# A two-layer graph network's message stage: TensorE's looped program written out straight, the hidden layer two groups ahead, fixed buffers for gathered rows

## The reference

```python
src, dst, x = ...            # 212,500 edges sorted by dst, 12,500 nodes, x: 12500 x 64
Wxh = x @ Wl.T + bl                                   # layer 0
h = silu(edge_attr @ Wf1.T + bf1)                     # edge_attr: 212500 x 64
f = h @ Wf2.T + bf2
agg = segment_sum(f * Wxh[dst], src, 12500)
x = layernorm(x + layernorm(x + agg) * gamma + beta)
agg = segment_sum(x[src] * edge_weight[:, None], dst, 12500)   # layer 1
x = layernorm(x + relu((agg + x) @ W1 + b1) @ W2 + b2)
```

## Time and profile before

| | |
|---|---|
| time, median of 3 runs | 4407.96 us (4403.15 to 4412.23) |
| profiled execution, its own time | 4366.64 us |
| its span, first to last instruction | 4364.9 us |
| VectorE, TensorE, GpSimd, ScalarE busy | 62%, 58%, 55%, 20% |
| first and last start of a scatter | 151.6 us, 3057.2 us |

### The profile page before, as it was taken

One profiled execution on the slowest core, in us unless ns is written; L12 is line 12 of the kernel. 1 busy time (PEld: TensorE's weight loads), 2 busy tenths in 40 slices (PEclk: granted clock), 3 DMA queues, 4 the chain that ended last, 5 costly groups with the idle time before them and its releaser, 6 DMA issues. The chain is left out here.

```text
span 4364.9 us, 81175 instructions
## 1 busy us (share of the span) xinstructions
PE 2517.8 (58%) x28074; PEld 2052.6 (47%) x28075; DVE 2725.6 (62%) x5354; ACT 888.6 (20%) x1671; POOL 2381.8 (55%) x2228
## 2 busy tenths in 40 slices
PE   3565665555565565665555655555475166666775
PEld 3454444444444444444444444444464155555763
DVE  5555555555555555555555555555566899997776
ACT  2111111111111111111111111111111355551002
POOL 0466666566565665655656656656122655554452
PEclk9677777777677676767767777776798555558998
DMA  7422222222222222222222222221686199999992
GB/s 213 96 68 68 68 68 63 64 69 67 61 70 64 65 71 61 69 66 61 68 67 61 69 65 67 69 61 51 234 332 250 57 306 303 305 306 354 406 406 96
DMA packets 205906, 585.25 MB, mean 134 GB/s; under 512 B 57272, under 2 KB 74432, under 8 KB 193216
## 3 DMA queue, kind: packets, MB, share of 16 engines
q1 hardware_dynamic: 134016, 369.03, 27.5%
q0 software_dynamic: 68336, 213.37, 13.4%
q10 hardware_dynamic: 3408, 0.92, 0.1%
HBM read 389.22 MB, written 194.13 MB: 134 GB/s over the span
## 5 line engine op out<-in xcount | busy, mean ns | idle before, releaser
L1019 POOL DMA_INDIRECT region_rows<-x_space,pos x1664 | 1797.4, 1080 | 1128.2 <-DVE x_space L972 632.2
L972 DVE TENSOR_TENSOR x_space<-rest,x_space 128x512 bf16<-128x512 f32 x208 | 144.0, 692 | 1010.2 <-issue 628.0
L886 PEld LDWEIGHTS ps_fx<-tmp_space,window 128*128 128x128 bf16 x9984 | 483.1, 116 | 532.1 <-issue 528.7
L868 PE MATMUL ps_rank<-onehot,tri 128*128 128x98 bf16 x1664 | 160.2, 265 | 872.0 <-DVE onehot L907 866.9
L886 PE MATMUL ps_fx<-tmp_space,window 128*128 x9984 | 521.7, 218 | 241.5 <-issue 238.9
L868 PEld LDWEIGHTS ps_rank<-onehot,tri 128*128 128x128 bf16 x1664 | 118.6, 128 | 933.2 <-DVE onehot L907 927.6
L880 PE MATMUL ps_th<-in_t,w_wf 128*128 128x512 f32 x416 | 424.6, 1124 | 0.0
L823 ACT ACTIVATE hid_t<-ps_th,w_bf 128x512 f32<-128x512 f32 x208 | 143.0, 687 | 1162.4 <-remote 699.4
L894 PE MATMUL ps_fx<-w_wf,hid_t 128*128 128x128 f32 x1664 | 318.5, 342 | 40.2 <-issue 35.9
L894 PEld LDWEIGHTS ps_fx<-w_wf,hid_t 128*128 128x128 f32 x1664 | 268.6, 240 | 55.8 <-issue 55.2
L818 ACT COPY in_t<-ps_th 128x512 f32<-128x512 f32 x208 | 121.9, 586 | 767.5 <-PE ps_th L861 551.5
(11 more groups left out here) (232 smaller groups left out, 4776.5 us busy)
## 6 DMA issues: line engine op xcount, KB each, us to landing
tmp_space<-region_rows SPq DMA_DIRECT2D x98, 882.0 KB, 6.6
run_rows<-agg SPq DMA_DIRECT2D x98, 873.0 KB
x_space<-key_rows SPq DMA_DIRECT2D x98, 576.0 KB
x_space<-rbf SPq DMA_DIRECT2D x208, 256.0 KB
rel_bc<-rel_rows SPq DMA_DIRECT2D x208, 256.0 KB
region_rows<-x_space,pos POOLq DMA_INDIRECT x1664
region_rows<-x_space SPq DMA_DIRECT2D x1, 14259.0 KB, 73.5
wxh_rows<-agg POOLq DMA_DIRECT2D x1, 3328.0 KB, 23.3
```

What stands on the lines that cost most here:

```text
L868: e.matmul(ps_rank[:, 0:NB], tri[:, :], onehot[j % 2][:, t, :], start=(t == 0), stop=(t == T - 1))
L886: last = e.matmul(ps_x[:, t * D:(t + 1) * D], window_t[:, h, t * P:(t + 1) * P], wxh[:, bass.ds(b + h, 1), c, :].rearrange("p b d -> p (b ...
L1019: e.indirect_dma_start(out=region_rows, out_offset=bass.IndirectOffsetOnAxis(ap=pos[j][:, t:t + 1], axis=0), in_=rows_f[j][:, t, :], in_of ...
```

## The change

Four things change in `sorted_messages`, all the rest stays.

1. TensorE's program is written out for all 208 groups instead of looping over passes.
2. Two small buffers, `near` and `sides`, two of each, are filled by ScalarE for a group (`nearby`): the six rows of parts of the two `wxh` blocks that the group needs (384 bf16 for each partition), and its 16 values of `ind`. TensorE's L886 and L874 products read these at fixed addresses. `nearby` reads the block number into a register on ScalarE.
3. TensorE's order for group g becomes: block products of g, node rows of g, transposes of g + 1, output layer of g, hidden layer of g + 1. ScalarE's becomes: `high_part` and `middle_part` of g, then `nearby`, `inputs` and `hidden` of g + 2.
4. VectorE's bias step (`filters`) is moved from the start of a group to behind `positions` of the group before.

```diff
@@ sorted_messages @@
-            found = carve(0, (S, T * RW // 2), (S, T * D), (2, T, D))
+            found = carve(0, (S, T * RW // 2), (S, T * D), (2, T, D), (2, PARTS * D), (2, T))
...
+            near = [a.bitcast(BF16) for a in found[2 * S + 2:2 * S + 4]]
+            sides = [a.bitcast(BF16).rearrange("p (t k) -> p t k", k=2) for a in found[2 * S + 4:2 * S + 6]]
...
+            def after(body, i, j, by=1):
+
+                body(i + (j + by) // S, (j + by) % S)
@@ block.scalar @@
-                    seed(e, ev, si, hw, mw)
+                    seed(e, ev, si, hw, mw, nr, sd)
+
+                    def nearby(i, j):
+                        b = e.value_load(base_i[0:1, bass.ds(i * S + j, 1)], min_val=0, max_val=NB - 1)
+                        e.wait_ge(xw, count_of(i, j, 2))
+                        e.copy(near[j % 2], wxh[:, bass.ds(b, 2), :, :].rearrange("p b c d -> p (b c d)")).then_inc(nr, 1)
+                        e.wait_ge(rk, count_of(i, j, 2))
+                        e.copy(sides[j % 2], ind[:, tiles(i, j), :]).then_inc(sd, 1)
...
-                    def steady(i, j):
-                        after(inputs, i, j)
+                    def parts(i, j):
                         high_part(i, j)
-                        after(hidden, i, j)
                         middle_part(i, j)
+
+                    for j in range(2):
+                        nearby(0, j)
+                        inputs(0, j)
+                        hidden(0, j)
+                    with e.Fori(0, passes - 1) as i:
+                        for j in range(S):
+                            parts(i, j)
+                            after(nearby, i, j, 2)
+                            after(inputs, i, j, 2)
+                            after(hidden, i, j, 2)
...
@@ block.tensor: the loop's body is split into functions and reordered @@
-                    with e.Fori(0, passes) as i:
-                        for j in range(S):
-                            b = e.value_load(base_i[0:1, bass.ds(i * S + j, 1)], min_val=0, max_val=NB - 1)
...
+                    def blocks(i, j, b):
...
+                        e.wait_ge(sd, count_of(i, j))
+                        for t in range(T):
+                            last = e.matmul(ps_pairs[0:NB, bass.ds(b, 2)], onehot[j % 2][:, t, :], sides[j % 2][:, t, :],
+                                            start=False, stop=False)
+                        last.then_inc(rk, 1)
+
+                    def nodes(i, j):
+                        e.wait_ge(nr, count_of(i, j))
+                        e.wait_ge(m, count_of(i, j, 1))
+                        e.wait_ge(wi, count_of(i, j))
+                        for t in range(T):
+                            for h in range(2):
+                                for c in range(PARTS):
+                                    last = e.matmul(
+                                        ps_x[:, t * D:(t + 1) * D], window_t[:, h, t * P:(t + 1) * P],
+                                        near[j % 2][:, (h * PARTS + c) * D:(h * PARTS + c + 1) * D],
+                                        start=(h == 0 and c == 0), stop=(h == 1 and c == PARTS - 1))
+                        last.then_inc(xw, 1)
...
+                    def steady(i, j, ahead):
+                        b = e.value_load(base_i[0:1, i * S + j:i * S + j + 1], min_val=0, max_val=NB - 1)
+                        blocks(i, j, b)
+                        nodes(i, j)
+                        if ahead:
+                            after(inputs, i, j)
+                        outputs(i, j)
+                        if ahead:
+                            after(hidden, i, j)
 
                     inputs(0, 0)
                     hidden(0, 0)
+                    for i in range(passes):
                         for j in range(S):
+                            steady(i, j, i * S + j + 1 < NG)
@@ block.vector @@
-                    def products(i, j):
+                    def filters(i, j):
                         e.wait_ge(m, count_of(i, j, 1))
                         e.wait_ge(f2, count_of(i, j))
                         e.tensor_tensor(f_s[:, :, :], ps_f[:, :].rearrange("p (t d) -> p t d", d=D),
                                         wts["bf2"][:, None, :].broadcast_to([P, T, D]), ALU.add).then_inc(f1, 1)
+
+                    def products(i, j):
                         e.wait_ge(hw, count_of(i, j, 2))
...
                         after(positions, i, j)
+                        after(filters, i, j)
```

More of the change, by code:

```diff
@@ L786, in sorted_messages @@
             gate = only_if(sorted_i, True)
-            def after(body, i, j):
-                body(i + (j + 1) // S, (j + 1) % S)
+            def after(body, i, j, by=1):
+                body(i + (j + by) // S, (j + by) % S)
             with nc.Block() as block:
@@ L854, in _ @@
                     e.matmul(ps_pairs[0:NB, 0:NBP], zeros[:, 0:NB], zeros[:, 0:NBP], start=True, stop=False).then_inc(f_zero, 1)
-                    with e.Fori(0, passes) as i:
-                        for j in range(S):
-                            b = e.value_load(base_i[0:1, bass.ds(i * S + j, 1)], min_val=0, max_val=NB - 1)
[L858 to L895, removed]
-                            last.then_inc(f2, 1)
@@ new lines, in inputs, with hidden @@
+                    def inputs(i, j):
+                        e.wait_ge(ld[j], i * 16 + 16)
+                        e.wait_ge(ev, count_of(i, j, 1))
+                        for t in range(T // 2):
+                            last = e.transpose(ps_t[:, t * P:(t + 1) * P],
+                                               rbf_s[j][:, t * P:(t + 1) * P], ident[:, :])
+                        last.then_inc(tr, 1)
+                    def hidden(i, j):
+                        e.wait_ge(si, count_of(i, j, 1))
+                        e.wait_ge(ev, count_of(i, j))
+                        e.matmul(ps_h[:, :], wts["wf1"][:, :], in_t[:, :], start=True, stop=True).then_inc(h1, 1)
@@ new lines, in blocks @@
+                    def blocks(i, j, b):
+                        e.wait_ge(rn, count_of(i, j, 1))
+                        e.wait_ge(oh, count_of(i, j))
+                        for t in range(T):
+                            e.matmul(ps_rank[:, 0:NB], tri[:, :], onehot[j % 2][:, t, :],
+                                     start=(t == 0), stop=(t == T - 1))
+                        for t in range(T):
+                            e.matmul(ps_cnt[:, 0:NB], ones[:, :], onehot[j % 2][:, t, :],
+                                     start=(t == 0), stop=(t == T - 1))
+                        e.wait_ge(sd, count_of(i, j))
+                        for t in range(T):
+                            last = e.matmul(ps_pairs[0:NB, bass.ds(b, 2)], onehot[j % 2][:, t, :], sides[j % 2][:, t, :],
+                                            start=False, stop=False)
+                        last.then_inc(rk, 1)
@@ new lines, in outputs @@
+                    def outputs(i, j):
+                        e.wait_ge(f1, count_of(i, j, 1))
+                        e.wait_ge(si, count_of(i, j))
+                        for t in range(T // 2):
+                            last = e.matmul(ps_f[:, t * P:(t + 1) * P], hid_t[:, t * P:(t + 1) * P],
+                                            wts["wf2"][:, :], start=True, stop=True)
+                        last.then_inc(f2, 1)
+                    def steady(i, j, ahead):
[7 more added lines that the diff above has]
+                            after(hidden, i, j)
@@ L897, in _ @@
+                    inputs(0, 0)
+                    hidden(0, 0)
+                    for i in range(passes):
+                        for j in range(S):
+                            steady(i, j, i * S + j + 1 < NG)
                     e.matmul(ps_pairs[0:NB, 0:NBP], zeros[:, 0:NB], zeros[:, 0:NBP], start=False, stop=True).then_inc(f_zero, 1)
@@ L987, in _ @@
                     positions(0, 0)
+                    filters(0, 0)
                     with e.Fori(0, passes - 1) as i:
```

16 lines of the change are left out of this document (7 added, 9 removed).

## The result

The changed kernel takes 4654.66 us (median of four runs, 4649.21 to 4666.01) beside 4405.56 of the kernel before in the same sets of runs: a ratio of 1.058, 95% interval 1.0533 to 1.0628. I forecast 3800 us, in 3680 to 4010, and a gain; the kernel got slower.

What follows compares the result with a forecast made beforehand. A ring of waits, 13.97 us a group, was taken as the bound, GpSimd's 11.07 as the next: 208 groups in 2303 us instead of 2906.6, minus 604, gives 3762.6, scaled to 3800 us; range 3680 to 4010.

Steps and rivals of the forecast that it cites:

- The ring of waits: Scatter stage: waits linking TensorE, ScalarE and VectorE pace the groups, 12.30 us in one group, 13.97 in the mean.
- The new ring: Scatter stage after the change: with the hidden layer out of the ring, 9.1 to 9.7 us a group.
- the 0.4 us before the rest part: New wait of VectorE's L968 for ScalarE's `high_part`, which queues behind the next group's Silu: 0.4 us.
- GpSimd's pace: Scatter stage: GpSimd's eight scatters a group become the next bound, 11.07 us a group.
- the stretching: Scatters lengthened where VectorE's L940 runs beside them: 0.78 us of GpSimd's time a group, taken as unchanged.
- TensorE straight: Scatter stage: writing out TensorE's program costs 0 in the sum, instruction supply being hidden beside GpSimd.
- fixed buffers: Register work ahead of L886 goes; ScalarE's two added copies, up to 2 us a group, cost the ring nothing.
- (a): TensorE's program straight, not looped: supply costs 0; 10 us stalls and L886 breaks ascribed to loop and registers.
- (d): GpSimd then sets the pace at 11.07 us a group; even with TensorE's stalls left, most of the gain stays.
- the store: Two or more groups finished ahead of GpSimd cover a 10 us TensorE stall, refilled by 1.5 to 2 us per group.
- Rival E: TensorE's stalls are no matter of loop or register and often eat GpSimd's store: 13.5 to 14 us a group; 6%.
- Rival D: The straight program starves TensorE of instructions: 18.2 us a group, 5290 us, if one in five comes slowly; 7%.

Runs made afterwards that it cites:

- a1: Changed kernel with GpSimd scattering one of a group's eight tiles, on chip 12: 3219.69 us.
- c1: The changed kernel itself, unaltered, on chip 4: 3732.84 us, ratio 0.9581 to the kernel before.
- b2: The kernel before, in its old order, with only TensorE's program written out straight, on chip 12: 3898.43 us.
- c2: Changed kernel with TensorE's new order as a loop over passes, on chip 4: 3741.73 us, ratio 0.9604 to the kernel before.
- d1: Changed kernel without its fixed buffers (register addresses again, no ScalarE copies), on chip 11: 3745.3 us, ratio 0.9596 to the kernel before.
- h1: Changed kernel with TensorE looped over passes and without the fixed buffers, so the new order alone, on chip 15: 4669.54 us.
- e2: Changed kernel with 45 extra matmuls on TensorE after the node rows once in twelve groups (17 times), on chip 1: 4865.2 us.
- i1: Changed kernel with a GpSimd memset of 3072 float32 per partition behind each group's eight scatters: 4534.88 us.
- j1: Changed kernel with a GpSimd memset of 1536 float32 per partition behind each group's eight scatters: 4161.19 us.
- g1: Changed kernel with GpSimd's 1664 scatters replaced by as many direct DMAs from SyncE, whose loads go three groups ahead, on chip 15: 3222.16 us.

## Why the prediction was wrong

**What held.** The ring of waits, and that it goes: 61 us of waits before the low part against 1010. The new ring was put at 9.1 to 9.7 us and is 8.48 (a1): the 0.4 us before the rest part isn't paid (a1's list of waits has no such row; in the recorded trace it is, 68.8 us in 100 waits), and the low part waits 0.3 a group, 60.0 us in all. GpSimd's pace was put at 11.07 and is 10.92 (c1), the stretching 0.63 a group for the forecast 0.78. That it comes from L940 alone was misread: in the trace of before the 192 scatters beside the node window (L915) take 1.339 us in the mean, in c1 the 206 beside the window take 1.355 and the 318 beside the old L940 1.135, where the rest take 0.987. "TensorE straight" and "fixed buffers" were priced at nothing and are worth 0 to 0.3% (b2, c2, d1). Where TensorE's stream flows, the forecast order of events is what the trace shows, and 3733 us is in my range, for the reasons given: the stage takes 2272 us for 2303, all else 1455 for 1460. Its base of 4407.96 was not that chip's, however: the gain there is 163 us, not 604, because the stage before took 11.7 us a group on such chips (b2) and not 13.97. So the size of the gain would have been off by nearly four times even with the sign right. I had measured GpSimd's 11.07 against a ring that was slowed by the stretches, and called the difference the change's gain.

**The step that failed** is (a)'s "The 10 us stalls and the breaks in L886 I take to belong to the loop and to the registers" with (d)'s "So even a change that leaves the stalls in place keeps most of the gain". Both took the stalls as given from outside, 15 in 208 groups. They belong neither to the loop nor to the registers: the changed kernel has neither in its node-row bursts and h1 has both, with the same stalls, and on chip 12 b2 has the registers and not one late start. Their number depends on the schedule. In the trace of the changed kernel slow stretches begin 5.6 us or more after a run of scatters (with breaks of at most 0.8 us) begins, never in its first microseconds, and they end with it: of the 941 late starts 938 lie within a run. The trace of before could have told it. There are 15 places, 12 groups apart, in which GpSimd scatters two groups without a break of over 1.5 us, and the 15 stalls lie in just these, each beginning about 14 us after the first scatter of the two groups. That of the earlier trace rows lies in this one:

```profile
1497.21 1.44 POOL L1019 DMA_INDIRECT region_rows<-x_space,pos  x1 [1.66 <-DVE x_space L972]
1500.07 0.98 POOL L1019 DMA_INDIRECT region_rows<-x_space,pos  x1 [1.43 <-issue]
...
1518.74 0.98 POOL L1019 DMA_INDIRECT region_rows<-x_space,pos  x1 [0.30 <-issue]
```

Of the short breaks in L886 (311 late starts in 186 groups) all but two come 6.9 us or more after the run began. The order of before made GpSimd wait, 1.6 to 2.4 us between most groups and 4.3 between some 50 (632 us on L972 in all), so its runs were mostly 10 to 11 us long. The new order delivers the second group of a pair while the first is being scattered, and the run becomes 21 us. TensorE is slow for the rest of that run, up to 16 us; GpSimd then runs dry for 9 us, which ends the run, and the pattern begins again: 9.2 + 21.5 = 30.7 us for two groups. That the store would carry GpSimd over a stall assumed stalls 12 groups apart; at one in two groups the 2.4 us regained per group never fill it, and e2 shows pauses paid in full. That the length of the run is the cause, and not only where the slow starts lie, is argued from these traces and was not shown: i1 and j1 were to show it and met the other kind of chip. Nor is length enough by itself: in c1 one run lasts the whole stage with no late start. Shown, by a single run each, are two things: without GpSimd's indirect DMAs there are none (g1), and with the new order alone they are as many as in the changed kernel (h1).

**Rival E** named this outcome and was under-priced in both ways: 6%, and 13.5 to 14 us a group for what is 15.33. I let it end where the kernel before stood, though nothing kept a stall that depends on the overlap from getting more frequent with it. Its sign and D's, "issue" ahead of TensorE's loads, is in the list of waits above: 664.2 us at L905. Rival D also had TensorE's instructions coming slowly and a slower kernel, but for the wrong reason (supply of a straight program). The Trainium skill, "Runtime: NRT & Kernel Launch", section "Instruction fetch mechanics", says that a taken branch whose target lies outside the current window of two pages has to fetch it first, and gives this as one reason to write programs out. b2 beside before shows nothing gained by it (3898.43 against 3890.35): in the looped kernel, with a body of four groups, the instruction queues bring nothing from 200 to 3000 us.

**What stays open.** What it is in GpSimd's indirect DMAs that slows another engine's instruction stream, and why on some chips only. The DMA engines are no busier where it is slow (share 0.21 in the recorded trace against 0.31 in c1). Whether the loads beside them have a part, whether shorter runs of scatters would cure it, and which part of the new order lengthens them wasn't settled either.

## What to carry to other kernels

When an engine starts instructions with fixed addresses and no waits at a fraction of its usual rate, ask what the other engines do at that time before calling it a stall from outside: a change that overlaps more may multiply it. A gain worked out as "now" minus "next bound" holds only if "now" does not itself contain such a loss. And compare a change on more than one chip before trusting its sign: here it is +5.8% where it was recorded and -4.2% on chip 4.

## What the runs showed of the hardware

Eight chips fell into two kinds with nothing between: 3889 to 3904 us (4, 7, 8, 11, 12, 14) and 4372 to 4394 (1, 15) for one and the same program. On the second kind TensorE's stream falls from 18 pairs of weight load and matmul per us (48 in 2.72) to 2 or 3 (24 from 1513.5 to 1523.7) while GpSimd issues indirect DMAs. SyncE's stream is touched too. A register move of its loop, at the load of the attributes, takes 29 ns every time on chip 4, and up to 392 in the recorded trace of the same kernel and 700 in that of before (duration in ns, minimum/median/maximum, of before and of chip 4):

```profile
L801 SPq MOVE x_space<-rbf x204: 4/29/700, 146.8 to 2986.5; - x102
```

```profile
L803 SPq MOVE x_space<-rbf x208: 29/29/29, 129.6 to 2347.8; - x104
```

VectorE, ScalarE and GpSimd go on undisturbed beside it: their register arithmetic and moves in the stage take at most 0.16 us in the recorded trace, as in c1, and L977, which starts at 1516.36 in the middle of a slow stretch, takes its usual 0.97. The stages behind take nearly the same time on both kinds: 4664.3 - 3340.4 = 1324 us behind the last scatter in the recorded run, 3727.0 - 2423.3 = 1304 on chip 4. TensorE's straight programs in them have no idle time of over 0.3 us put down to "issue" in either trace.
